# Slot inputs turned on VectorE and moved by DMA instead of transposed on TensorE

## What is computed

```python
logits = jnp.einsum('bnd,des->bnes', x_n, mu_n)          # B=2, N=2048, D=512, E=16, S=128
dispatch = jax.nn.softmax(logits, axis=1)
combine = jax.nn.softmax(logits.reshape(B, N, E * S), axis=-1)
slot_in = jnp.einsum('bnd,bnes->besd', x_ln, dispatch)
h = jax.nn.gelu(jnp.einsum('besd,edh->besh', slot_in, W1) + b1[None, :, None, :], approximate=False)
slot_out = jnp.einsum('besh,ehd->besd', h, W2) + b2[None, :, None, :]
out = jnp.einsum('bsd,bns->bnd', slot_out.reshape(B, E * S, D), combine)
```

## Time and profile before

| | us |
|---|---|
| median of 3 runs | 2524.89 |
| lowest and highest | 2522.9, 2526.19 |
| profiled execution | 2528.95 |
| its span | 2527.2 |
| PE busy, share of the span | 2424.3, 96% |
| DVE, ACT, POOL busy | 1735.4, 1429.6, 1608.0 |
| mean granted TensorE clock | 0.969 |

### The profile page before, as it was taken

How to read it: one execution, slowest core, us unless ns; L and a number is a source line. 1 busy time by engine, 2 the same in 40 slices (tenths; PEclk the granted TensorE clock), 3 DMA queues, 4 the chain that set the end, 5 groups by cost and what they waited for, 6 DMA issues and landing times. The chain is left out here.

```text
span 2527.2 us, 38816 instructions
## 1 busy us (share of the span) xinstructions
PE 2424.3 (96%) x12834; PEld 1731.1 (68%) x12834; DVE 1735.4 (69%) x3805; ACT 1429.6 (57%) x2764; POOL 1608.0 (64%) x1747
## 2 busy tenths in 40 slices
PE   8989999999999999996988999998999997999998
PEld 6875555555555555543767888887888886788886
DVE  3338888888888888843876656567656564767776
ACT  3214566766666666663865656566656563454553
POOL 4402577777878777677957676665675765555554
PEclk9987999999999999998989999999999998999999
DMA  7862466565747566545965445477444457674553
GB/s 245 272 204 60 97 132 132 125 140 115 150 102 154 111 139 130 123 99 156 353 199 155 154 140 164 130 228 193 143 151 153 142 161 248 188 225 133 148 151 102
DMA packets 249177, 400.87 MB, mean 159 GB/s; under 512 B 57712, under 2 KB 112016, under 8 KB 237584
## 3 DMA queue, kind: packets, MB, share of 16 engines
q1 hardware_dynamic: 195856, 283.47, 36.7%
q0 software_dynamic: 52480, 114.37, 20.5%
q10 hardware_dynamic: 640, 0.55, 0.1%
HBM read 180.63 MB, written 112.22 MB: 116 GB/s over the span
## 5 line engine op out<-in xcount | busy, mean ns | idle before, releaser
L1033 ACT ACTIVATE p_probs<-p_ps_s 128x512 f32<-128x512 f32 (+3 forms) x1280 | 591.5, 541 | 316.5 <-PE p_ps_s L955 304.0
L1624 POOL DMA_DIRECT2D p_eT<-p_ex x1024 | 538.5, 535 | 272.5 <-DVE p_ex L1890 221.0
L1064 DVE TENSOR_REDUCE p_parts<-p_ps_m 128x1 f32<-128x512 f32 x768 | 468.2, 679 | 69.5 <-PE p_ps_m L942 69.2
L955 PE MATMUL p_ps_s<-q,k_e 98*128 98x512 f32 (+3 forms) x1280 | 470.4, 388 | 3.3 <-ACT p_probs L1033 3.1
L942 PE MATMUL p_ps_m<-k_m,q 96*128 96x512 f32 (+3 forms) x1280 | 456.0, 393 | 9.5 <-PEq L2165 3.9
L884 POOL TENSOR_TENSOR p_added<-p_added,p_probs 128x2048 f32<-128x2048 f32 x88 | 419.0, 4764 | 31.2 <-ACT p_probs L1033 17.4
L955 PEld LDWEIGHTS p_ps_s<-q,k_e 98*128 98x128 f32 x1280 | 243.3, 192 | 181.4 <-ACT p_probs L1033 77.0
L942 PEld LDWEIGHTS p_ps_m<-k_m,q 96*128 96x128 f32 x1280 | 246.5, 196 | 94.1 <-DVE p_parts L1068 25.0
L973 PE MATMUL p_ps_c<-p_probs,v_e 128*32 128x512 f32 (+3 forms) x2560 | 285.9, 547 | 7.2 <-POOL p_probs L864 7.0
L2024 POOL TENSOR_TENSOR p_acc<-p_acc,logit 128x512 f32<-128x512 f32 x112 | 164.0, 1465 | 150.9 <-ACT logit L2077 147.2
L1068 DVE CUSTOM_DVE_ANT_0 p_masked<-p_ps_m,p_mask 128x384 f32<-128x384 f32 (+3 forms) x512 | 217.9, 485 | 36.8 <-PE p_ps_m L942 32.3
(11 more groups left out here) (194 smaller groups left out, 4869.2 us busy)
## 6 DMA issues: line engine op xcount, KB each, us to landing
p_probs<-p_probs POOLq DMA_DIRECT2D x56, 1024.0 KB, 7.7
logits_t<-logit SPq DMA_DIRECT2D x32, 1024.0 KB, 5.0
p_eT<-p_ex POOLq DMA_DIRECT2D x1024, 32.0 KB, 2.1
logit<-logits_t SPq DMA_DIRECT2D x128, 256.0 KB, 3.5
q<-q_t SPq DMA_DIRECT2D x96, 256.0 KB, 4.8
c_first<-L_ffn_W_dram SPq DMA_DIRECT2D x64, 256.0 KB, 5.7
p_probs<-p_probs POOLq DMA_DIRECT2D x16, 768.0 KB, 7.4
p_x<-L_attn_x_dram SPq DMA_DIRECT2D x32, 256.0 KB, 5.6
```

Source lines behind the costliest of these rows:

```text
L955: pe.matmul(ps_s[:, u % ST_BANKS, q0:BLK], k_e[:, bass.ts(kt, P)], q[:, qb, h, q0:BLK], start=True, stop=True).then_inc(s_score, 1)
L1033: act.activation(probs[s % RING][:, h, q0:BLK], ps_s[:, u % ST_BANKS, q0:BLK], ACT.Exp).then_inc(s_exp, 1)
L1064: dve.tensor_reduce(to, bank, AX.X, ALU.max).then_inc(s_taken, 1)
L1624: pool.dma_start(eT[r][p * QD:(p + 1) * QD, i, :, :], ex[i * QD:(i + 1) * QD, 2 * r:2 * r + 2, bass.ts(p, P)]).then_inc(s_eT[r], 16)
```

## The change

`slot_in_t` goes away. In its place VectorE turns `si` in 32x32 blocks where it stands (`turn_slot_in`, first in its pass), and SyncE moves the blocks with 16 transfers of 32 partitions x 4 x 32 elements, 16 KB each, into `siT_lo` (`move_slot_in`, second in its pass, behind `load_mu` and ahead of everything else). ScalarE and VectorE then make `siT_hi` and `siT_lo` out of `siT_lo` in SBUF, no longer out of `ps_e`. For the last unit half of the transfers go on GpSimd's queue, ahead of its loads for the next stage. On TensorE `hidden` moves behind product 1 and `slot_out` behind product 2. ScalarE's `slot_in_hi` moves behind exp 1, and `gelu` ahead of exp 3; VectorE's `slot_in_lo`, `hidden_lo` and `bias` move accordingly.

```diff
@@ block.sync
+            def move_slot_in(n):
+                sp.wait_ge(s_sT, n + 1)
+                if n > 0:
+                    sp.wait_ge(s_h, n)
+                for q in range(NQ if n < UNITS - 1 else NQ // 2):
+                    for a in range(NQ):
+                        sp.dma_start(siT_lo[q * QD:(q + 1) * QD, :, a * QD:(a + 1) * QD].bitcast(F32),
+                                     si[a * QD:(a + 1) * QD, :].rearrange("p (c q j) -> p c q j", q=NQ, j=QD)[:, :, q, :]).then_inc(s_siT, 16)
...
-            walk([(0, load_mu)] + [(0, load_unit_rows(j)) for j in range(JG)]
+            walk([(0, load_mu), (3, move_slot_in)] + [(0, load_unit_rows(j)) for j in range(JG)]
@@ block.gpsimd, after the moves of all units
+            pool.wait_ge(s_sT, UNITS)
+            pool.wait_ge(s_h, UNITS - 1)
+            for q in range(NQ // 2, NQ):
+                for a in range(NQ):
+                    pool.dma_start(siT_lo[q * QD:(q + 1) * QD, :, a * QD:(a + 1) * QD].bitcast(F32),
+                                   si[a * QD:(a + 1) * QD, :].rearrange("p (c q j) -> p c q j", q=NQ, j=QD)[:, :, q, :]).then_inc(s_last, 16)
@@ block.tensor
-            def slot_in_t(n):
-                pe.wait_ge(s_si, n + 1)
+            def hidden(n):
+                pe.wait_ge(s_wlo, 2 * n + 1)
+                pe.wait_ge(s_sTlo, n + 1)
                 if n > 0:
                     pe.wait_ge(s_add, n)
...
-                for c in range(DC):
-                    mm = pe.transpose(ps_e[:, 0, bass.ts(c, P)], si[:, bass.ts(c, P)], ident[:, :])
-                mm.then_inc(s_sT, 1)
...
-            walk([(1, logits(0)), (3, slot_in_t), (1, logits(1)), (1, logits(2)), (3, hidden),
-                  (1, logits(3)), (3, slot_out), (2, product(0)), (2, product(1)), (2, product(2)), (1, largest_t),
-                  (2, product(3)), (2, largest_rows)])
+            walk([(1, logits(0)), (1, logits(1)), (1, logits(2)), (1, logits(3)), (2, product(0)), (2, product(1)),
+                  (3, hidden), (2, product(2)), (3, slot_out), (1, largest_t), (2, product(3)), (2, largest_rows)])
@@ block.scalar
             def slot_in(n):
...
-                    act.wait_ge(s_sT, n)
+                    act.wait_ge(s_siT, 256 * n)
...
             def slot_in_hi(n):
-                act.wait_ge(s_sT, n + 1)
+                if n < UNITS - 1:
+                    act.wait_ge(s_siT, 256 * (n + 1))
+                else:
+                    act.wait_ge(s_siT, 256 * n + 128)
+                    act.wait_ge(s_last, 128)
...
-                act.activation(siT_hi[:, :, :], ps_e[:, 0, :], ACT.Copy).then_inc(s_sThi, 1)
+                act.activation(siT_hi[:, :, :], siT_lo[:, :, :].bitcast(F32), ACT.Copy).then_inc(s_sThi, 1)
@@ block.vector
+            def turn_slot_in(n):
+                dve.wait_ge(s_si, n + 1)
+                dve.transpose(si[:, :], si[:, :]).then_inc(s_sT, 1)
...
-            walk([(3, slot_in_lo), (1, maximum(0)), (1, largest(0)), (1, maximum(1)), (2, split_lo(0)), (1, largest(1)), (2, rows_lo(0, False)),
+            walk([(3, turn_slot_in), (1, maximum(0)), (1, largest(0)), (1, maximum(1)), (2, split_lo(0)), (1, largest(1)), (2, rows_lo(0, False)),
```

More of the change, by code:

```diff
@@ L1500, in slots @@
         s_sum, s_rs, s_turn, s_ehi, s_elo, s_prod = (sem(n) for n in ("sum", "inverse", "turned", "e_hi", "e_lo", "product"))
[L1501 removed]
+        s_si, s_sT, s_sThi, s_sTlo = sem("slot_in"), sem("slot_in_turned"), sem("slot_in_hi"), sem("slot_in_lo")
+        s_siT, s_last = sem("slot_in_moved"), sem("last_slot_in_moved")
         s_h, s_g, s_hhi, s_hlo, s_o = sem("hidden"), sem("gelu"), sem("h_hi"), sem("h_lo"), sem("slot_out")
@@ L1672, in slot_in_t @@
                         pe.wait_ge(s_mrow, n // E)
-                for c in range(DC):
-                    mm = pe.transpose(ps_e[:, 0, bass.ts(c, P)], si[:, bass.ts(c, P)], ident[:, :])
-                mm.then_inc(s_sT, 1)
-            def hidden(n):
-                pe.wait_ge(s_wlo, 2 * n + 1)
-                pe.wait_ge(s_sTlo, n + 1)
                 for c in range(DC):
@@ L1813, in largest_row @@
                     act.dma_start(d["top"][n // E], m_row[:, :]).then_inc(o_m, 16)
-            walk([(3, slot_in), (1, copy(0)), (3, slot_in_hi), (1, copy(1)), (2, split_hi(0)), (2, rows_hi(0, False)),
-                  (1, copy(2)), (3, gelu), (2, rows_hi(1, False)), (2, split_hi(1)), (1, copy(3)), (2, rows_hi(2, False)), (0, vectors_hi), (1, exp(0)), (1, exp(1)),
-                  (2, split_hi(2)), (2, rows_hi(3, False)), (1, exp(2)), (1, exp(3)), (2, split_hi(3)),
+            walk([(3, slot_in), (1, copy(0)), (1, copy(1)), (2, split_hi(0)), (2, rows_hi(0, False)),
+                  (1, copy(2)), (2, rows_hi(1, False)), (2, split_hi(1)), (1, copy(3)), (2, rows_hi(2, False)), (0, vectors_hi),
+                  (1, exp(0)), (1, exp(1)), (3, slot_in_hi),
+                  (2, split_hi(2)), (2, rows_hi(3, False)), (1, exp(2)), (2, split_hi(3)), (3, gelu), (1, exp(3)),
                   (0, unit_rows_hi(0)), (0, unit_rows_hi(1)), (3, out_hi),
@@ L1921, in largest_col @@
                         dve.tensor_reduce(m_col[:, group(j)], ps_l[:, j, :].rearrange("p (t s) -> p t s", t=TG), AX.X, ALU.max).then_inc(s_mc, 1)
-            walk([(3, slot_in_lo), (1, maximum(0)), (1, largest(0)), (1, maximum(1)), (2, split_lo(0)), (1, largest(1)), (2, rows_lo(0, False)),
-                  (1, maximum(2)), (3, hidden_lo), (2, rows_lo(1, False)), (2, split_lo(1)), (1, maximum(3)), (3, bias), (2, rows_lo(2, False)),
-                  (0, vectors_lo), (1, largest(2)), (1, turn(0)), (1, turn(1)), (2, split_lo(2)), (2, rows_lo(3, False)), (1, turn(2)), (1, turn(3)),
-                  (2, split_lo(3)), (0, unit_rows_lo(0)),
+            walk([(3, turn_slot_in), (1, maximum(0)), (1, largest(0)), (1, maximum(1)), (2, split_lo(0)), (1, largest(1)), (2, rows_lo(0, False)),
+                  (1, maximum(2)), (2, rows_lo(1, False)), (2, split_lo(1)), (1, maximum(3)), (2, rows_lo(2, False)),
+                  (0, vectors_lo), (1, largest(2)), (1, turn(0)), (1, turn(1)), (3, slot_in_lo), (2, split_lo(2)),
+                  (2, rows_lo(3, False)), (1, turn(2)), (2, split_lo(3)), (3, hidden_lo), (1, turn(3)),
+                  (3, bias), (0, unit_rows_lo(0)),
                   (1, largest(3)), (0, unit_rows_lo(1)), (1, total), (3, out_lo), (1, largest_col), (0, unit_rows_lo(2)), (0, unit_rows_lo(3))]
```

3 lines of the change are left out of this document (1 added, 2 removed).

## The result

The changed kernel takes 2559.09 us (median of 4 runs, 2558.24 to 2560.89) where the kernel before takes 2525.54 beside it: a ratio of 1.0131, 95% interval 1.0118 to 1.0144. It is slower, as forecast, but by 33.6 us and not by 6, and 13 us outside the range. The profiled execution after has a span of 2556.5 us against 2527.2.

The account below looks back on a forecast made before the run. TensorE was taken to bound the kernel. Terms -11.4 + 2.0 + 1.6 + 2.1 + 0.3 + 4.8 + 6.4 = +5.8 us on the median 2524.89 gave 2530.7, say 2531, range 2518 to 2546.

Parts of the forecast that it names:

- 26 steady rounds: Slots-stage passes 3 to 15 and 19 to 31: removing four TensorE transposes saves 0.44 us each, -11.4 us.
- round 17: Slots-stage pass at the change of batch: late turn and moves start the first layer at 18.7, not 16.6; +1.6 us.
- round 18: Slots-stage pass at the change of batch: moves queue behind row loads, stores and vectors' load, landing at 25.4; +2.1 us.
- round 33: Near the slots stage's end: unit 30's moves wait behind SyncE's 16 loads; TensorE idles 9.5 us; +4.8 us.
- round 34, copy to high half: Unit 31 at the stage's end: turn and eight moves on each of two queues take 7.8 against 1.4; +6.4 us.
- a tie: Stage's end: GpSimd's 16 loads land near 46.3 after unit 30's product, the layers' chain ends at 47; no term.
- the threshold of 0.66 us an issue: SyncE's moves in every round: issue cost, from (14.5 - 4.0)/16, that decides whether they come late.
- the price of an issue: SyncE's 16 moves a unit: 0.43 us each, 6.9 us in all (6.6 to 9.8).
- 1 (the gain stays): SyncE's queue does not hold unit 15's and unit 30's moves: -7.2 us, 2518; chance 0.14.
- 2 (the cover of 0.4 us fails): Slack before the first layer in steady rounds fails; TensorE waits up to 0.6 us a round, 2531 to 2546; chance 0.14.
- 3 (late in every round): Moves cost 1.0 us an issue, the high half comes 5.5 late in every round: +130, 2660; chance 0.05.
- 4 (the stall is only displaced): The four transposes only displaced a stall, the round stays at 24.65: +17 us; chance 0.03.

Follow-up runs that it names:

- the 24 moves of the experiment: The changed kernel with eight of each unit's 16 moves cut in two, 24 transfers a unit; 2752.89 us, ratio 1.0901.
- The four forms: The changed kernel with each unit's four destination quarters filled from slot inputs or DRAM, in 128- or 512-byte runs; 2558.53 us in one run.
- the order alone: The changed kernel's order, but all 32 units' slot inputs transposed on TensorE again, no turn or moves; 2540.12 us, ratio 1.0051.

## Why the prediction was wrong

Term by term, over the stage (differences after minus before):

| term | forecast | measured |
|---|---|---|
| 26 steady rounds | -11.4 | -11.8 |
| rounds 1 and 2 | 0 | +0.5 |
| round 16 | +2.0 | +3.0 |
| round 17 | +1.6 | +9.4 |
| round 18 | +2.1 | +6.9 |
| round 32 | +0.3 | +0.5 |
| round 33 | +4.8 | +10.0 |
| round 34, copy to high half | +6.4 | +9.2 |
| from there to the next stage | 0 ("a tie") | +6.7 |
| sum | +5.8 | +34.4 |

**Right.** The direction; the steady rounds, to a few hundredths, with a cover of 0.67 us where 0.4 was laid out (in round 15 the high half came 0.79 late and the first layer 0.12); the places of all losses but the last; and the threshold of 0.66 us an issue, nearly. Read from the trace it is a train of 10.8 us or 0.67 an issue: the high half is wanted at 14.44, the moves begin at 2.43, and the last lands 1.2 behind the end of its train. The median train is at 0.65, six of 26 lie above 0.67 and cost next to nothing, and the 24 moves of the experiment show what lies well beyond it. Part of this was luck: the prediction added the landing of the earlier trace rows to the end of the last issue, where the row counts from its start. That is some 0.5 us too much and stood against an issue priced too low.

**The step that failed first is the price of an issue, above all in a full queue.** It was taken as 0.43 from the load of `q`, which resembles the move in partitions and runs per partition. The four forms show that neither decides: what that load has and the move has not is a source in DRAM with long runs. The other row, 0.61, from SBUF in 128-byte runs, was the right neighbour. And no single price holds: 0.64 in the steady round, 0.68 in rounds 17 and 33 and at the change of batch 1.01, behind 16 loads of 256 KB, as the one full-queue row had hinted (1.02). Against 6.9 us for 16 moves these are 10.9, 10.9 and 16.2: 4.0 us more in rounds 17 and 33 each, and 9.3 in round 18. The price alone is not enough, though. With 0.61 the prediction's own terms give 2.9 more in each of these rounds, +14.5 in all and inside its range. Of the 28.6 us that are missing, rounds 17, 18 and 33 have 17.8, round 34 has 2.8 and the last stretch 6.7.

**The second is what a wait costs behind itself.** The prediction charged 1.3 us for the lower clock in round 33, from the first layer alone. The product block behind it runs at 1.2 GHz too: 7.42 us for work of 4.12. That is 3.3 in round 17, where nothing was charged. For round 17 it closes the account: 1.6 forecast, 4.5 for the later first layer (23.2 instead of 18.7: the moves took 4.0 longer and began 1.2 later, behind ScalarE's wait for the weights, and 0.7 of that came back in the landing), 3.3 for the clock, 9.4. The weights are late because unit 13's moves and the 16 loads of unit rows stand ahead of them in SyncE's queue, which the prediction did not charge; with unit 14 back on TensorE the round is still 7.2 longer, and with no moves at all it is 24.7 as before. In round 33 the first layer came 4.5 later than laid out, 4.0 of it the moves, and the product block behind it ran 1.0 longer at the lower clock; the rest of the round was 0.3 shorter. That makes the 5.2 that were missing.

**Round 18.** The moves began at 10.8 and not at 16.5, since the loads of rows began 1.3 earlier and took 8.43 and the store took 2.14 and not 3.9 us; they took 16.2 and not 6.9, and ended at 27.0. The first layer started at 29.8 (forecast 26.9), and 11.0 us followed where 9.1 were laid out. Two errors of opposite sign hid the larger. Of the round's +6.9, 5.8 are there without any move (the order alone): SyncE's hold at `b2` makes the vectors' load late by itself, and ScalarE waits 4.00 us for it in that version.

**Round 33 and the order.** The loads of stored outputs did start and end where the prediction put them (they end 7.4 us behind unit 30's product). The order alone costs 8.3 us over rounds 32 to 34, of which the prediction had charged 0.3; it saw these loads late, but counted only the moves behind them and not the weights of unit 31, for which ScalarE waits 8.86 us in that version. With the moves ahead of the weights ScalarE has the longer wait for the moves and none for the weights. The moves add 18.1 to the 8.3.

**Round 34.** 2.8 us more than forecast. GpSimd's moves, issued at the forecast rate (0.54 each), began 2.98 us behind SyncE's though both wait for the same turn, and the last landed 10.6 after the copy. SyncE's eight took 0.70 each, and their last landed at 10.1. Laid out were 7.8, so either queue was over 2 us late.

**The tie was none, and this is the third step that failed**: a term put at nothing. GpSimd's loads were to land at 46.3 after unit 30's product and the layers' chain to end at 47. The last landed at 56.7 and the chain was done at 53.6. Behind the landing stood GpSimd's DRAIN of 3.3 us, which the prediction did not have; in the kernel before one of 2.7 ran hidden. 3.2 us to the landing, 0.2 from there and 3.3 of DRAIN make the 6.7.

**Rivals.** 1 (the gain stays) fell with the gaps in rounds 18 and 33. 2 (the cover of 0.4 us fails) did not happen, though it was nearer than it looked: in round 15 ScalarE's 0.7 us of waiting used up the cover and 0.12 more. 3 (late in every round) needed more than 0.67 an issue in every round and had it in six of 26. 4 (the stall is only displaced) is refuted by the round of 24.19. Even the high ends of the sum, worked with 0.61 an issue, gave +20: in the crowded rounds an issue cost more than that, and each later first layer then ran at the lower clock too.

## What to carry to other kernels

Price a transfer by a row with the same kind of source and the same run length, count its landing from where the row counts it, and then look for it in the fullest place of its queue, not in a quiet one: the same move cost 0.64, 0.68 and 1.01 to 1.15 us here. A gain that comes in equal parts from many quiet rounds can be kept if the few crowded rounds are left as they were; look for these first, and let them fall back. Where an instruction that a queue waits for is moved, count what stands behind it in that queue before counting the operation itself: here about 14.6 of 34 us came from SyncE standing behind one late result. And before a chain is called hidden, add what its engine does after its last transfer has landed.
